# A gated cross-attention and mixture-of-experts kernel: the last group by halves, rows turned before they are scaled, router logits of three blocks on VectorE

## The reference, cut to what matters

```python
x = x + tanh(g_xattn[0]) * L0_xattn(layernorm(x), ctx)     # softmax attention, then Wo, bo
x = x + tanh(g_ffn[0])   * L0_ffn(layernorm(x))            # shared SwiGLU + top-1 of 8 routed SwiGLU
x = x + tanh(g_xattn[1]) * L1_xattn(layernorm(x), ctx)     # softmax attention, then an MLP:
                                                           #   relu(o @ W1 + b1) @ W2 + b2
x = x + tanh(g_ffn[1])   * L1_ffn(layernorm(x))            # below
def L1_ffn(x):
    logits = x @ Wg + bg;  top 2 of 8;  w = softmax(top 2)
    mixed = sum over the two of w * (relu(x @ W1[e] + b1[e]) @ W2[e] + b2[e])
    return layernorm(mixed + x) * gamma + beta
```

## Time and profile before

| | us |
|---|---|
| median of 3 runs | 1487.17 (1486.02 to 1487.17) |
| profiled execution | 1488.32 |
| its span | 1486.5 |
| TensorE busy | 1352.8 (91%) |
| ScalarE busy | 982.6 (66%) |
| VectorE busy | 539.6 (36%) |
| GpSimd busy | 175.0 (12%) |

### The profile page before, as it was taken

The page is one execution under the profiler, slowest core; times in us unless marked ns, Lnnn a source line. Parts: engine busy times, 40 slices in busy tenths (PEclk is TensorE's granted clock), DMA queues, the critical chain, the costliest instruction groups (busy, mean ns, idle before and its releaser), DMA issues. The chain is left out here.

```text
span 1486.5 us, 31922 instructions
## 1 busy us (share of the span) xinstructions
PE 1352.8 (91%) x13236; PEld 715.3 (48%) x13236; DVE 539.6 (36%) x1204; ACT 982.6 (66%) x1178; POOL 175.0 (12%) x188
## 2 busy tenths in 40 slices
PE   7799999999999996999869999999999985399994
PEld 4433333333333653899733334334334323299983
DVE  7412142241433253333461123322422433644435
ACT  4499999999997233222259995995995980155532
POOL 2000000000000330233300000000000000166530
PEclk9899999999999998999978999999999997599997
DMA  7671010101001814111338010110111215012223
GB/s 208 157 125 27 20 27 20 27 20 27 23 20 28 294 57 151 58 50 47 104 110 149 20 28 14 34 27 16 34 27 47 65 33 167 18 62 75 72 67 157
DMA packets 65867, 100.82 MB, mean 68 GB/s; under 512 B 10075, under 2 KB 47967, under 8 KB 64953
## 3 DMA queue, kind: packets, MB, share of 16 engines
q1 hardware_dynamic: 59768, 82.47, 20.5%
q0 software_dynamic: 5952, 16.26, 3.4%
HBM read 67.99 MB, written 26.21 MB: 63 GB/s over the span
## 5 line engine op out<-in xcount | busy, mean ns | idle before, releaser
L1232 ACT ACTIVATE arena<-ps 128x1024 f32<-128x1024 f32 x556 | 554.5, 1224 | 56.7 <-PE ps L998 56.7
L998 PE MATMUL ps<-arena 99*32 99x512 bf16 x6656 | 465.5, 384 | 16.8 <-PEq L848 10.9
L998 PEld LDWEIGHTS ps<-arena 99*32 99x32 bf16 x6656 | 149.8, 95 | 408.5 <-issue 168.2
L1232 ACT ACTIVATE wqkv<-ps 128x1024 f32<-128x1024 f32 x276 | 294.9, 1225 | 22.7 <-PE ps L998 22.7
L1014 PE MATMUL ps<-arena 128*32 128x512 f32 x2224 | 289.7, 593 | 1.3 <-ACT arena L1232 0.8
L1314 DVE COPY work<-ps 128x512 f32<-128x512 f32 x32 | 22.1, 691 | 406.6 <-PE ps L1014 406.6
L1704 PEld LDWEIGHTS ps<-work,arena 128*128 128x128 f32 x1184 | 145.1, 196 | 6.4 <-DVE work L1801 3.4
L1704 PE MATMUL ps<-work,arena 128*128 128x128 f32 x1184 | 146.2, 279 | 2.1 <-DVE work L1801 2.1
L1014 PE MATMUL ps<-wqkv,arena 128*32 128x512 f32 x1104 | 143.9, 593 | 0.0
L1905 POOL DMA_INDIRECT work<-xn_img,fetch x62 | 60.3, 973 | 613.4 <-POOLq L978 596.8
L1716 PE MATMUL ps<-arena,work 128*128 x496 | 117.2, 380 | 0.0
(11 more groups left out here) (206 smaller groups left out, 1158.7 us busy)
## 6 DMA issues: line engine op xcount, KB each, us to landing
arena<-in_ew SPq DMA_DIRECT2D x16, 512.0 KB, 5.6
arena<-q_img SPq DMA_DIRECT2D x32, 192.0 KB
arena<-y_tok SPq DMA_DIRECT2D x12, 512.0 KB, 6.3
arena<-k_img SPq DMA_DIRECT2D x8, 624.0 KB, 13.3
q_img<-work SPq DMA_DIRECT2D x18, 256.0 KB, 2.5
k_img<-work SPq DMA_DIRECT2D x21, 208.0 KB, 2.5
arena<-q_img SPq DMA_DIRECT2D x32, 128.0 KB
work<-work SPq DMA_DIRECT2D x128, 32.0 KB, 1.9
```

Source lines behind the costliest of these rows:

```text
L998: last = nc.tensor.matmul(ps[i * VW:(i + 1) * VW, buf + j, :], k2[0:ROWS + SHIFT, h, at:at + VW], q2[0:ROWS + SHIFT, h, :], start=True, st ...
L1232: nc.scalar.activation(probs[(b * STEPS + u) % RING], ps[:, buf:buf + 2, :], ACT.Exp, scale=SCALE).then_inc(s_exp, 1)
```

## The change

1. **Last group by halves** (both layers). `last_group` leaves out the copy from PSUM and takes reciprocal and product by halves of 256 columns; the product reads the bank. `gather_last` sends each half as soon as it is there; the second is counted on a new semaphore s_oh2.
2. **Last projection by halves** (layer 1). Hidden and output run for 256 columns and then for the other 256.
3. **The last block's tail** (layer 1) becomes `own_tail`. The bias b2 times the gate is added to x before the last group. Statistics are taken pair by pair. The rows are first only reduced by their mean and released to be turned; the Newton iteration follows, then the rows are scaled for the store. The logits are scaled by the reciprocal root when they are read.
4. **Logits of blocks 0 to 2 on VectorE** (layer 1). TensorE's turns and logits in the steps are gone. VectorE multiplies the normed rows with each expert's router row and reduces, four experts behind group 1 and four behind group 2. The router rows are loaded, spread to all partitions, into ctxT's place, first on SP's queue.

```diff
-        ctxT = sb("ctxT", [CH + 1, 2, MP])
+        ctxT = sb("ctxT", [P, 2, MP])
+        router_rows, at = view(over_ctx, 0, [E, D])
+        router_prod, at = view(over_ctx, at, [TB, D])
...
-            NU = NO + 3
+            NU = NO + (3 if l == 0 else 0)
...
+                        if b == NB - 1 and half == 0:
+                            pe.wait_ge(s_on, NB * NG + 1)
+                        if b == NB - 1 and t == 2:
+                            pe.wait_ge(s_oh2, 16 * HG)
...
-                                route(b, w)
+                                if l == 0:
+                                    route(b, w)
...
                     def last_projection():
+                        for half in range(2):
+                            cols = slice(half * 2 * P, (half + 1) * 2 * P)
+                            if half:
+                                pe.wait_ge(s_oh2, 16 * HG)
+                            else:
+                                for i in range(2):
+                                    pe.wait_ge(s_oc[i], NB * 16 * HG * NG // 2)
+                                pe.wait_ge(s_on, NB * NG)
+                            for f in range(4):
+                                if half:
+                                    pe.wait_ge(s_read7, use(NB, f))
+                                for k in range(KD):
+                                    last = nc.tensor.matmul(ps[:, f, cols], w1[:, k, f * P:(f + 1) * P], oT[:, k, cols],
+                                                            start=(k == 0), stop=(k == KD - 1), skip_group_check=True)
+                                last.then_inc(s_full7, 1)
+                        for half in range(2):
+                            if half:
+                                pe.wait_ge(s_on, NB * NG + 1)
+                            for f in range(4):
+                                pe.wait_ge(s_read7, use(NB, 4 * half + f))
+                                for t in range(2 * half, 2 * half + 2):
+                                    last = nc.tensor.matmul(ps[:, 4 + t, 0:D], hidT[:, f, t * P:(t + 1) * P], w2[:, f, :],
+                                                            start=(f == 0), stop=(f == 3))
+                            last.then_inc(s_full7, 1)
...
+                    def last_group():
+                        g, n = NG - 1, NB * NG
+                        dve.wait_ge(s_pv, NB * NG * NC)
+                        nc.vector.stream_shuffle(out=sums, in_=ps[:, 6 + g % 2, :], mask=[DH] * VW).then_inc(s_copy, 1)
+                        dve.wait_ge(s_copy, n)
+                        for i in range(2):
+                            cols = slice(i * 2 * P, (i + 1) * 2 * P)
+                            nc.vector.reciprocal(sums[:, cols], sums[:, cols]).then_inc(s_inv, 1)
...
+                            nc.vector.tensor_tensor(o_norm[:, g % 2, cols], ps[:, 6 + g % 2, cols], sums[:, cols],
+                                                    ALU.mult).then_inc(s_on, 1)
...
+                    def own_tail():
+                        last_group()
+                        for half in range(2):
+                            cols = slice(half * 2 * P, (half + 1) * 2 * P)
+                            for f in range(4):
+                                dve.wait_ge(s_full7, use(NB, 4 * half + f))
+                                nc.vector.tensor_scalar(hidT[:, f, cols], ps[:, f, cols], b1[:, f:f + 1], 0.0,
+                                                        ALU.add, ALU.max).then_inc(s_read7, 1)
+                        for pair in range(2):
+                            dve.wait_ge(s_full7, use(NB, 8 + pair))
+                            nc.vector.scalar_tensor_tensor(out=rows, in0=ps[:, 4 + 2 * pair:6 + 2 * pair, 0:D], scalar=tg,
+                                                           in1=rows, op0=ALU.mult, op1=ALU.add).then_inc(s_xup[pair], 1)
+                            dve.wait_ge(s_xup[pair], NB)
+                            for i in range(2 * pair, 2 * pair + 2):
+                                nc.vector.bn_stats(stats[:, i, :], x[:, (NB - 1) * TB + i, :])
+                        dve.drain()
+                        step(norm_means(TB))
+                        for i in range(TB):
+                            last = nc.vector.tensor_scalar(xn[:, (NB - 1) * TB + i, :], x[:, (NB - 1) * TB + i, :],
+                                                           mv[:, i, 0:1], None, ALU.subtract)
+                        last.then_inc(s_ends, 1)
+                        norm_newton(step, TB)
+                        dve.wait_ge(s_rt, 1)
+                        for i in range(TB):
+                            last = nc.vector.tensor_scalar(xn[:, (NB - 1) * TB + i, :], xn[:, (NB - 1) * TB + i, :],
+                                                           rstd[:, i:i + 1], None, ALU.mult)
+                        last.then_inc(s_xs, 1)
...
+                    def logits(b, es):
+                        for e in es:
+                            step(nc.vector.tensor_tensor(router_prod, xn[:, rows, :], router_rows[:, e, :].unsqueeze(1)
+                                                         .broadcast_to([P, TB, D]), ALU.mult))
+                            step(nc.vector.tensor_reduce(lg[:, rows, e], router_prod, AX.X, ALU.add))
...
+                        elif b == NB - 1:
+                            for t in range(TB):
+                                last = nc.vector.scalar_tensor_tensor(out=lg[:, b * TB + t, :], in0=got_logits[:, t, :],
+                                                                      scalar=rstd[:, t:t + 1], in1=rb[:, :],
+                                                                      op0=ALU.mult, op1=ALU.add)
...
                         group(b, 1)
-                        if b:
+                        if b and l == 0:
                             turned(b - 1)
                             route(b - 1)
+                        elif b:
+                            logits(b - 1, range(E // 2))
                         group(b, 2)
-                    tail(NB, NB - 1)
+                        if b and l == 1:
+                            logits(b - 1, range(E // 2, E))
+                            route(b - 1)
+                    if l == 1:
+                        for pair in range(2):
+                            rows = x[:, (NB - 1) * TB + 2 * pair:(NB - 1) * TB + 2 * pair + 2, :]
+                            nc.vector.scalar_tensor_tensor(out=rows, in0=b2[:, :, :], scalar=tg, in1=rows, op0=ALU.mult,
+                                                           op1=ALU.add)
+                        dve.drain()
+                        own_tail()
+                    else:
+                        tail(NB, NB - 1)
...
+                    if l == 1:
+                        sp.dma_start(router_rows.rearrange("p e d -> p (e d)"), spread(a["rt1"], E * D)).then_inc(s_rr, 16)
...
-                    gather_heads(NB - 1, NG - 1)
+                    gather_last()
...
-                        sp.wait_ge(s_ends, NB)
+                        sp.wait_ge(s_xs, 1)
                         store_rows(NB - 1)
```

More of the change, by code:

```diff
@@ L1161, in last_projection @@
                     def last_projection():
-                        for i in range(2):
-                            pe.wait_ge(s_oc[i], NB * 16 * HG * NG // 2)
-                        pe.wait_ge(s_u, NB * NG)
-                        for f in range(4):
-                            for k in range(KD):
-                                last = nc.tensor.matmul(ps[:, f, :], w1[:, k, f * P:(f + 1) * P], oT[:, k, :],
-                                                        start=(k == 0), stop=(k == KD - 1))
-                            last.then_inc(s_full7, 1)
@@ L1170, in last_projection @@
-                        for f in range(4):
-                            pe.wait_ge(s_read7, use(NB, f))
-                            for t in range(TB):
-                                last = nc.tensor.matmul(ps[:, 4 + t, 0:D],
-                                                        hidT[:, f, t * P:(t + 1) * P], w2[:, f, :],
-                                                        start=(f == 0), stop=(f == 3))
-                                if f == 3 and t % 2 == 1:
-                                    last.then_inc(s_full7, 1)
+                        for half in range(2):
[13 more added lines that the diff above has]
+                                last.then_inc(s_full7, 1)
@@ L1327, in tail @@
                     def tail(b, now, first_group=None):
-                        group(now, NG - 1)
+                        if b == NB:
+                            last_group()
+                        else:
+                            group(now, NG - 1)
                         k = 0
-                        own = L.mlp and b == NB
                         if L.mlp:
@@ L1340, in tail @@
                             nc.vector.tensor_tensor(y_tmp.rearrange("p (t d) -> p t d", d=D),
```

(8 more changed lines are left out.)

38 lines of the change are left out of this document (33 added, 5 removed).

## The result

Measured: 1473.71 us, median of four runs (1471.56 to 1476.74), against 1486.6 (1484.9 to 1487.17) of the kernel before; ratio 0.9916 [0.9903, 0.9928], by which it is 12.5 us less, between 10.7 and 14.4. Forecast were 1470.8 us and 16.4 us less. Direction, range and the kind of each gain were right; the sum was 2 to 6 us too large.

A forecast was written before the change was run, and what follows sets the result against it. ScalarE was taken to set layer 1's attention pace, TensorE having nearly no slack, with a serial chain behind. Gains 8.55 + 2.48 + 5.28 - 0.2 + 0.3 = 16.4 us, from 1487.17 to 1470.8 us; range 1466.5 to 1477.

The forecast's parts named there:

- Part 1: Layer 1's attention: taking three blocks' transposes and logits off TensorE returns ScalarE's waits, 2.85 us per block, 8.55 us gained.
- VectorE's cover: VectorE's added logits fit its idle time at 1.22 us per reduction, leaving 5.8 us in middle blocks, 2.0 in the last.
- Part 2: Router rows' broadcast on SP's queue ahead of groups 1 to 3's queries and keys: cost 0, upper bound 5 us.
- Part 3: Layer 1's last group: no copy ahead, reciprocal and product by halves, so the first issue comes earlier; 2.48 us gained.
- Part 4: Last hidden layer and output by halves: splitting adds no time, first 3.6 us stay at clock 0.52; gain 0.
- Part 5: Behind the last output: statistics earlier, Newton beside TensorE, transposes after 3.25 us; 5.28 us gained, 0.2 lost on logit scaling.
- Part 6: Layer 0's last group, halved too: at most 0.3 us gained, since TensorE has shared-expert work there.
- the clock stays up: Rival: layer 1's last transposes and logits run at full clock, a further 2.6 us gained, 1468.2 us; 22%.
- The late keys: Rival: group 1's keys arrive late behind the router rows, up to 5 us lost, 1475.8 us; 8%.
- the unreturned time: Rival: TensorE's freed time isn't returned because another wait is late next; only 7.9 us gained, 1479.3 us; 4%.
- the open loads: Rival: the 16 added weight loads of the halved projection stand in the open, 4.2 us, 1475.0 us; 1%.
- the overrun: Rival: VectorE's logits outlast its idle time and delay the groups; at 1.2 us more per operation 1492.0 us, slower; 3%.

The follow-up runs named there:

- e1: Kernel before with only the logits of three blocks moved to VectorE and the router rows' load added: 1481.19 us.
- e4: Changed kernel with the hidden layer's and output's pieces one step of keys later in layer 1: 1472.61 us.
- e3: Changed kernel with each of the four router products of the second half done twice in all three blocks: 1477.98 us.
- e7: Changed kernel with the last group of both layers normalised and copied whole instead of by halves: 1475.08 us.
- e11: Changed kernel with 14 matmuls that nobody reads added behind the last block's first MAX8 in layer 1: 1469.86 us.
- e10: Changed kernel with e4, e9 and e11 together, and 2 more unread matmuls before the counts: 1462.24 us.
- e9: Changed kernel with 7, 3 and 1 unread matmuls before the last hidden layer, the transposes and the logits: 1469.04 us.
- e6: Changed kernel with Newton and the full scaling back ahead of the last block's transposes in layer 1: 1476.19 us.
- c_after: The changed kernel run again unaltered: 1472.58 us.
- e8: Changed kernel with the router rows' load issued by GpSimd instead of SyncE: 1473.88 us.
- e5: Changed kernel with 12, 5 and 1 unread matmuls before the last hidden layer, the transposes and the logits: 1470.46 us.

## Why the prediction was right, and where it was off

- **Part 1, 8.55 us: the mis-sized term.** Measured 5.56 in the profiles of before and after, 5.1 with e1. The mechanism, TensorE's extra work showing as ScalarE's waits, was right; two things in the sum were not.
  - *Pace read from starts.* The earlier trace rows hold the durations 3.78, 4.08 and 3.86. By the ends, 24 exponentials took 1177.29 - 1155.29 = 22.00 us undisturbed and 1201.62 - 1177.29 = 24.33 with TensorE's extra work: 2.33 a block, 7.0 in all. The profile calls 2.05 of each 2.33 a wait (0.38 and 1.67); the rest is no wait: the exponentials right behind a wait take some 0.1 us longer. The rows needed for this were in the prediction; I used only their first column.
  - *A longer wait before hidden*, 1.06 us in the block of [3.26] and 0.35 in the next, 1.4 in all: 7.0 - 1.4 = 5.6. I had treated that wait as a constant, and why the copies land later isn't shown. e4's profile shows that the wait is paid in full. In e1 it took 0.9 us, and the early wait 0.8: 7.0 - 1.8 = 5.2, beside its 5.1.
- **VectorE's cover** was right to 0.3 us: 1.22 us per operation, 5.56 and 2.25 us of idle time left, and e3 shows what happens beyond them.
- **Part 2** (router rows) right at 0: in the kernel after ScalarE has no wait in the first 97 us behind its first exponential, and group 1's scores begin some 24 us into that. In e7, e11 and e10 there was one wait of 0.19 to 0.66 us some 32 us behind the first exponential, whose cause no run shows.
- **Part 3, 2.48 us:** issue 3.11 us behind the shuffle, as worked out. From issue to hidden it was 3.68 instead of 3.90: 0.2 more gained. e7 confirms the halving.
- **Part 4, 0:** wrong by 0.8 us in this execution. The clock's first part was carried over from the earlier trace rows as if it were a property of the place; in the nine profiles of the halved tail without added matmuls ahead of it hidden took 8.72 to 10.11 us, where the earlier trace rows have 8.78. The rule of the Trainium skill (TensorE: Matmul & The Clock Gate, The mechanism) on weight loads would leave every load in the open; e9's 32 passes beside 32 loads at 0.223 us each disagree with it again.
- **Part 5, 5.28 us:** right. Last output to transposes 3.30 us (8.53 before); e6 isolates Newton's share. The four logit scalings cost 0.43, not 0.2.
- **Part 6:** 0.23 of 0.3.
- **Rivals.** The clock stayed down at transposes in the first profile (1.97 us); in c_after, e7, e8 and e11 they took 1.09, logits still at the lower level. So the rival "the clock stays up" was half real, and is a matter of the execution, 0.9 us and not 2.6. That the first profile had it down is luck, as far as the runs show: the same kernel had it up in c_after. The late keys, the unreturned time, the open loads and the overrun didn't occur.
- **The sum.** 5.56 + 6.67 + 0.23 = 12.5 us are the change's by the profiles, the same as the measured 12.5. That they agree so closely is partly luck: c_after, the same kernel, came out at 14.7 by its ratio, and the clock of one execution moves its tail alone by 1.5 us. The rest of the profiles' 15.3, 2.6 ahead of attention 1 and 0.3 behind MAX8, lies where the change does nothing, and the kernel before and e1 differ by 3.0 in the first of these places with the same instructions.

## What to carry over

Read an engine's pace from the ends of its instructions (start plus duration) over a long undisturbed piece: starts alone can run ahead. Before pricing what a faster engine gains, look at each wait of its partner for a DMA: if it reaches such a wait with no slack, the wait must be moved along (here one step of keys later, 3.9 us in the profile). And in a serial tail, matmuls that nobody reads, cut to just less than TensorE's idle time, held the clock at its upper level here and were worth 3.4 us there (e9); cut too long, they cost what they overrun (e5).

## What the runs showed of the hardware

- ScalarE's recorded starts run ahead by up to 0.6 us after a stall: the group of four grows from 3.78 to 4.41 us and stays there.
- An f32 matmul of 128x512 makes two records and takes 0.88 us at a granted clock of 1.0.
- TensorE idle for 6.87 us or more came back at a granted clock of 0.50, and the same hidden layer then took 8.72 to 10.11 us by the execution, 7.14 at the upper level. After 3.30 us of idle time the transposes ran at the upper level in four executions and at the lower in four. Idle times of 0.68 and 0.73 us between added and real matmuls did no such harm.
- SyncE's four issues for a group take 2.41 us mostly and 2.5 to 3.6 at some gathers, not moved by taking a load off its queue. The cause is open.
